# Where the summed arguments of an RNN's and an LSTM's tanhs are kept: SBUF or spare PSUM columns

## What is computed

```python
# 1: RNN, 512 wide, over the 1024 steps
next_h = jnp.tanh(xw_t + prev_h @ Wh)
# 2: a diagonal state-space layer with a short convolution, then a projection
# 3: LSTM, 512 wide, over the 1024 steps
A = xw_t + prev_h @ Wh
i, f, o = (sigmoid(A[:, k*512:(k+1)*512]) for k in range(3));  g = tanh(A[:, 1536:])
next_c = f * prev_c + i * g
next_h = o * jnp.tanh(next_c)
# 4: a matrix per sequence (base layer plus a product of low rank) applied to every step
```

## Time and profile before

| | before |
|---|---|
| median of three runs | 3935.61 us |
| span of the profiled execution, first to last instruction | 3932.7 us |
| TensorE (PE) matmuls busy | 3630.1 us, 92% |
| VectorE (DVE) busy | 3273.3 us, 83% |
| ScalarE (ACT) busy | 1748.5 us, 44% |
| GpSimd (POOL) busy | 774.4 us, 20% |
| mean granted TensorE clock | 0.995 of full speed |

### The profile page before, as it was taken

The page is one execution under the profiler, slowest core; times in us unless marked ns, Lnnn a source line. Parts: engine busy times, 40 slices in busy tenths (PEclk is TensorE's granted clock), DMA queues, the critical chain, the costliest instruction groups (busy, mean ns, idle before and its releaser), DMA issues.

```text
span 3932.7 us, 255334 instructions
## 1 busy us (share of the span) xinstructions
PE 3630.1 (92%) x110596; PEld 3058.0 (78%) x110596; DVE 3273.3 (83%) x19155; ACT 1748.5 (44%) x8244; POOL 774.4 (20%) x3623
## 2 busy tenths in 40 slices
PE   7899999999999999999999999999999999999875
PEld 4688788888888788888888888888888888877654
DVE  6588888888888888888888888888888888888766
ACT  4244444444444444444444444444444444444432
POOL 0122222222222222222222222222222222212111
PEclk9899999999999999999999999999999999999999
DMA  7100000000000000000000000000000000000000
GB/s 275 48 7 7 10 10 10 7 7 10 10 10 9 9 7 7 10 10 10 10 7 7 10 10 10 10 7 10 7 10 10 10 10 7 7 7 7 7 6 8
DMA packets 19109, 63.32 MB, mean 16 GB/s; under 512 B 3958, under 2 KB 4526, under 8 KB 14914
## 3 DMA queue, kind: packets, MB, share of 16 engines
q1 hardware_dynamic: 17692, 46.67, 3.7%
q10 hardware_dynamic: 294, 0.33, 0.0%
HBM read 38.48 MB, written 8.39 MB: 12 GB/s over the span
## 4 chain that ended last, share of the span: by engine, by line
DVE 55%; PE 39%; issue 4%; ACT 1%; SPq 1%; DMA 0%; ACTq 0%; DVEq 0%; POOL 0%; POOLq 0%
PE ps_lstm L1027 32%; DVE lstm_sums L745 19%; DVE lstm_arg L750 8%; DVE lstm_ig_fc L756 7%; DVE lstm_gates_2c L761 5%; DVE rnn_sums L854 5%; DVE lstm_h_parts L785 3%; DVE lstm_h_scaled L778 2%; DVE lstm_h_parts L781 2%; PE ps_rnn L1066 2%; PE ps_lstm_in_b L1108 1%; PE ps_lstm_in_a L1171 1%; PE ps_ssm L1108 1%; SPq L301 1%; DVE rnn_h_parts L900 1%
## 5 line engine op out<-in xcount | busy, mean ns | idle before, releaser
L1027 PE MATMUL ps_lstm<-lstm_Wh_parts,lstm_h_parts 128*20 128x256 f16 x65472 | 1973.3, 273 | 259.4 <-DVE lstm_h_parts L785 246.8
L1027 PEld LDWEIGHTS ps_lstm<-lstm_Wh_parts,lstm_h_parts 128*20 128x20 f16 x65472 | 1543.1, 91 | 665.2 <-DVE lstm_h_parts L785 509.9
L487 ACT ACTIVATE lstm_gates_2c<-lstm_arg 128x32 f32<-128x32 f32 x2048 | 469.8, 229 | 1354.7 <-DVE lstm_arg L750 1354.7
L745 DVE STREAM_TRANSPOSE lstm_sums<-ps_lstm 128x256 f32<-128x256 f32 x2048 | 912.2, 445 | 191.5 <-PE ps_lstm L1027 157.4
L351 POOL COPY lstm_sums<-lstm_in 128x32 f32<-128x32 f32 x2048 | 423.7, 210 | 1749.8 <-DVE lstm_arg L750 1749.8
L1066 PE MATMUL ps_rnn<-rnn_Wh_parts,rnn_h_parts 128*20 128x128 f16 x32736 | 638.8, 220 | 22.4 <-DVE rnn_h_parts L900 20.3
L1066 PEld LDWEIGHTS ps_rnn<-rnn_Wh_parts,rnn_h_parts 128*20 128x20 f16 x32736 | 549.5, 92 | 56.2 <-DVE rnn_h_parts L900 38.5
L750 DVE TENSOR_REDUCE lstm_arg<-lstm_sums 128x32 f32<-128x96 f32 x2048 | 537.9, 263 | 35.2
L496 ACT ACTIVATE lstm_tanh_c<-lstm_gates_2c 128x8 f32<-128x8 f32 x2048 | 410.4, 200 | 253.7 <-DVE lstm_gates_2c L761 253.7
L510 ACT ACTIVATE rnn_h<-rnn_arg 128x16 f32<-128x16 f32 x1024 | 220.9, 216 | 515.8 <-DVE rnn_arg L859 515.7
L492 ACT ACTIVATE lstm_o_scaled<-lstm_gates_2c 128x8 f32<-128x8 f32 x2048 | 428.0, 209 | 33.4
(11 more groups left out here) (186 smaller groups left out, 2654.3 us busy)
## 6 DMA issues: line engine op xcount, KB each, us to landing
layer_plus_2I<-in_L_cond_w SPq DMA_DIRECT2D x16, 1024.0 KB, 6.3
out<-out_rows SPq DMA_DIRECT2D x128, 64.0 KB, 1.6
x_rows<-in_x SPq DMA_DIRECT2D x31, 256.0 KB
lstm_Wx<-in_L_cond_Wh SPq DMA_DIRECT2D x1, 4096.0 KB, 17.6
lstm_Wx<-in_L_cond_Wx SPq DMA_DIRECT2D x1, 4096.0 KB, 13.5
layer_plus_2I<-in_L_cond_Wh SPq DMA_DIRECT2D x1, 1024.0 KB, 9.5
rnn_Wx<-in_L_cond_Wx SPq DMA_DIRECT2D x1, 1024.0 KB, 11.7
lstm_in<-in_L_cond_w SPq DMA_DIRECT2D x1, 1024.0 KB, 10.1
```

The costliest lines, as they stand in the source:

```text
L487: A.activation(gate[h][:, 0:G, :].rearrange("p g q -> p (g q)"), arg[h][:, :, :].rearrange("p g n -> p (g n)"), ACT.Tanh, scale=gate_scale ...
L745: return mark(V.transpose(tr[h][s % 2][:, :, 0:QC], psL[h][:, 0:HW].rearrange("p (g c) -> p g c", c=QC)))
L1027: ins = mm(psL[h][QC * j:QC * j + LO + NB, 0:HW], hls[:, k, :], whl[:, k, h, e, j, :], start=(k == 0 and e == 0), stop=(k == KB - 1 and e ...
```

## The change

The SBUF tiles `rnn_arg` and `lstm_arg0/1` go. In their place the RNN's arguments take 16 columns of `ps_rnn` behind the 128 that matmuls write, and the arguments of both LSTM halves take 32 columns each of `ps_lstm0` behind the 256 that matmuls write. VectorE's reduces write there, and ScalarE's tanhs read there. No instruction, wait or order is added or removed.

```diff
-        arg_r = sb("rnn_arg", [P, KB, NB])
...
-        arg = [sb(f"lstm_arg{h}", [P, HG, NB]) for h in range(NH)]
...
+        arg_r = psR[:, RW:RW + KB * NB].rearrange("p (g n) -> p g n", n=NB)
+        arg = [psL0[:, HW + h * HG * NB:HW + (h + 1) * HG * NB].rearrange("p (g n) -> p g n", n=NB) for h in range(NH)]
...
                 def gates(h, s):
                     act.wait_ge(S[f"lstm_summed{h}"], s + 1)
-                    A.activation(gate[h][:, 0:G, :].rearrange("p g q -> p (g q)"), arg[h][:, :, :].rearrange("p g n -> p (g n)"),
+                    A.activation(gate[h][:, 0:G, :].rearrange("p g q -> p (g q)"), psL0[:, HW + h * HG * NB:HW + (h + 1) * HG * NB],
                                  ACT.Tanh, scale=gate_scale).then_inc(S[f"lstm_gated{h}"], 1)
...
-                        A.activation(hr[:, :, s, :], arg_r[:, :, :], ACT.Tanh, scale=rnn_scale).then_inc(S["rnn_tanh"], 1)
+                        A.activation(hr[:, :, s, :], arg_r, ACT.Tanh, scale=rnn_scale).then_inc(S["rnn_tanh"], 1)
...
-                    V.tensor_reduce(arg[h][:, :, :], three.rearrange("p g s n -> p g n s"), AX.X, ALU.add
+                    V.tensor_reduce(arg[h], three.rearrange("p g s n -> p g n s"), AX.X, ALU.add
                                     ).then_inc(S[f"lstm_summed{h}"], 1)
...
-                    V.tensor_reduce(arg_r[:, :, :], three.rearrange("p g s n -> p g n s"), AX.X, ALU.add).then_inc(S["rnn_summed"], 1)
+                    V.tensor_reduce(arg_r, three.rearrange("p g s n -> p g n s"), AX.X, ALU.add).then_inc(S["rnn_summed"], 1)
```

## The result

The changed kernel takes 3908.52 us (median of 4 runs, 3902.77 to 3910.64) against 3935.61 us (a fourth run of the kernel before took 3925.05 us; the median stays); the ratio of the runs is 0.9936, with a 95% interval of 0.9922 to 0.9950. It is faster by 0.5% to 0.8%, some 20 to 31 us, about half of the 51 us that were forecast. The profiled execution's span is 3900.9 us.

The account below looks back on a forecast made before the run. The prediction took the turn between VectorE and TensorE, 1024 steps, as the bound. Half 0's 15 to 20 ns plus half 1's 35 gave 0.050 us x 1024 = 51 us off 3935.6: 3884 us; range 3866 to 3987.

Parts of the forecast that it names:

- What bounds the kernel: VectorE and TensorE take turns in the LSTM loop: 3.62 us a turn, 1024 steps, 3707 us of the span.
- (1) ScalarE reads PSUM: The tanh reads its argument from PSUM: 35 ns less of 229, with 27 and 45 as ends.
- (2) VectorE writes PSUM: The reduce writes to PSUM: same duration, 0.26 us; the write lands 0.05 us later or 0.01 earlier at the ends.
- (3) The RNN: The RNN's reduce and tanh lie beside other work; in 64 steps without an LSTM 2 us at most, left out.
- reduce(1) and new_cell(0) follow it: In each LSTM step, both VectorE instructions were to start earlier along with products(0), by 15 to 20 ns.
- half 0's term: Per step, gates(0) ends 35 ns earlier but products(0) can use only 15 to 20, since transpose(1) is late next.
- TensorE's room: In the tightest step, L1129's matmuls end at about 1382.71 and L1027 starts at 1382.78: 0.07 us of room, still enough.
- tanh_cell(0) doesn't hold up h_part(0): Late in the step, a shorter gates(1) lets ScalarE start tanh_cell(0) earlier by the same 35 ns, so h_part(0) isn't delayed.
- a late write: Rival: each reduce into PSUM releases its tanh 50 ns later; +31 us in all, 3966 us; chance 0.15.
- The third: Rival: no reading gain for 32 elements, or the write eats it; time stays at 3936 us, 3925 to 3943; chance 0.12.
- The change of memory as a hold: Rival: VectorE's next instruction waits 0.045 us when the output memory changes; some 82 us more, 4018 us; chance 0.13.

Follow-up runs that it names:

- the run with the short transpose: Changed kernel, but transpose(1) takes only the first 4 of 8 blocks of half 1 in the loop's chunks; all three tiles in PSUM; one run, 3885.65 us.

## Why the prediction was wrong

The forecast was 3884 us, with 3869 to 3901 from the sum's own ends; measured are 3908.5. The direction and the mechanism of the saving were right; the size was about double what was measured.

- **What bounds the kernel:** right, the turn between TensorE and VectorE, 1024 times; the gain came from there.
- **(1) ScalarE reads PSUM:** right. Forecast 35 ns of 229, between 27 and 45; measured 32, and 33 for the RNN's. The fixed part is what falls, as the two pairs of the earlier trace rows said, down to 16 elements. The estimate from the page "VectorE: DVE Perf Modes" of the Trainium skill, 43 ns, is too large by a third for the tanh's own duration. The next ScalarE instruction does gain it: tanh_cell(0) started 0.136 us after gates(1) and now starts 0.093 after it (medians; 2004.22 to 2004.35 in the earlier trace rows, 1991.81 to 1991.90 after the change), 0.043 sooner.
- **(2) VectorE writes PSUM:** the same duration was taken, with 9 ns more in the lower end of the sum. Measured are 8 more. That is a mis-sized term: half 1 is worth 32 - 8 = 24 ns a step, not 35, so 11 us of the forecast's 51 went there.
- **(3) The RNN:** right. It is hidden in the steps with an LSTM (3.618 us a turn with it alone).
- **"reduce(1) and new_cell(0) follow it":** this sentence of the sum is the step that failed. products(0) did come 15 ns earlier (1.029 us after transpose(0) in place of 1.044, medians); reduce(1) did not, because it waits for transpose(1). That took the whole of half 0's term, 15 to 20 ns a step, of which the sum of 50 holds 15: 15 us. The two steps together are the gap between 51 us and the 25 measured, to within the noise. The instruction was bound twice, by its place behind products(0) and by its wait, within 0.01 us, and the rows showed both: 2003.92 is 0.09 after 2003.83 and 0.03 after 2003.89.
- **TensorE's room:** the 0.07 read off was about 0.005. From the start of L1129's last matmul to L1027 the median in steps 6 and 7 was 0.210 us before, when L1027 still waited for lo_part(0), and is 0.205 now, when it waits for L1129; the spacing of the matmuls ahead, 0.125, did not tell that. It cost about 1 us.
- **tanh_cell(0) doesn't hold up h_part(0):** the conclusion is wrong by a few ns, the reason behind it held. h_part(0) starts 0.032 to 0.033 us (median) after tanh_cell(0)'s end, before, after and in every other run (1992.10 to 1992.14 after the change), which is also the distance of products(1) from the end of gates(1): so it waited for tanh_cell(0) already before. products(1) would let it in only about 5 ns sooner (it starts 98 ns after products(1) starts, where 176 - 83 = 93 is the place of an instruction that waits for nothing). The number held because tanh_cell(0) moved along with gates(1), as the prediction said: it starts 43 ns sooner after it, as said above, and lasts 9 longer (192 to 201 ns). That this makes 34, the 35 of the sum, is luck.
- **The rivals:** a late write was right in kind, 8 ns and not 50, and so too small to turn the sign. The third was wrong: the reading gain is there for 32 and for 16 elements. The change of memory as a hold is refuted: transpose(1) starts 0.18 after reduce(0) and new_cell(0) 0.17 to 0.18 after reduce(1), as before. So the 0.045 that the memsets lose does not carry over to the reduces and the instructions behind them. The rule of the Trainium skill, page "VectorE: DVE Perf Modes", section on two Vector instructions with no wait between them, agrees: a change of memory alone held nothing. The Trainium skill's other figure, on that page in the section on the TRN2 errata, is 120 fixed cycles with PSUM as source against 58; carried over to a PSUM output, as the rival did, it did not show: the reduce grew by 8 ns, not 65, and the distance to the next instruction stayed at 0.18.

## What to carry to other kernels

Before a gain is carried from one instruction to the next, list every wait of that next instruction with its own time, also where the instruction ahead in the queue already explains its start; where two reasons lie within a few hundredths of a microsecond, the gain can end there. In this loop a fixed cost saved on the hop from VectorE to ScalarE counted only in half 1, where the instructions beside the tanh either had time to spare or moved along with it. Price both ends of a move: the reader's side gained 32 ns and the writer's side gave 8 back.

## What the runs showed that was not expected

A reduce into PSUM lasts 8 ns longer by its row, yet the next instruction starts no later (0.179 us from start to start in median, before and after): the longer end falls into the part that overlaps with the next instruction, and only an instruction on another engine that waits for the reduce pays it (the tanh starts 0.034 after the reduce's end, before and after). A tanh that reads PSUM lasts 32 ns less and lets the next ScalarE instruction in 43 ns sooner. Memsets lose about 0.045 us each way when the memory changes, and the instructions behind the reduces lose nothing. And a reduce that follows products(0) without having to wait for the transpose is 7 ns shorter than one that waits (264 against 271 ns, both into PSUM, in the run with the short transpose).
